# Two merged edits in a Swin block: scores of heads 4 and 5 spread over the whole array, and the narrow half of the second MLP product in rounded passes

## The chip, the cores and the metric

The kernel runs on one core of a Trainium2 chip. The metric is the device time of one execution in microseconds. A core has TensorE (PE, with its weight loads listed apart as PEld), VectorE (DVE), ScalarE (ACT), GpSimd (POOL), and SyncE (SP), which here only issues DMAs. Each engine runs its instructions in order; they meet at semaphores.

## What is computed

One transformer block with shifted 7x7 windows on an input of 16 x 56 x 56 x 192, in float32:

```python
xn = layernorm(x, ln1_w, ln1_b); xs = jnp.roll(xn, (-3, -3), (1, 2))
qkv = windows(xs) @ qkv_w + qkv_b                      # 1024 windows, 49 tokens, 6 heads of 32
attn = softmax(einsum('bhqd,bhkd->bhqk', q, k) * 32 ** -0.5)
o = einsum('bhqk,bhkd->bhqd', attn, v) @ proj_w + proj_b
x = x + roll(unwindow(o), (3, 3), (1, 2))
h = gelu(layernorm(x, ln2_w, ln2_b) @ mlp_w1 + mlp_b1)  # 192 -> 768
out = x + h @ mlp_w2 + mlp_b2                           # 768 -> 192
```

## The kernel before, in words

The work is cut into 128 groups, each a row of eight windows: 392 tokens, held as 4 blocks of 98. `body(i, parity)` of every engine handles the attention of group i and the MLP of group i - 1. `iterations` writes the first three bodies and the last ones out and puts the others, in pairs, into a hardware loop. There is no scheduler: the order on each engine is the order of the calls in its `body`, and the waits are written by hand.

Most products are done in float32 that is split in two. A value is rounded to `float32r` (the high part, by ScalarE or GpSimd) and the rest is the low part (by VectorE or GpSimd); three passes, high x high, high x low and low x high, one record of the trace each, stand for a float32 product. Other products (scores, probabilities times values, the transposes, and the narrow MLP half before) are plain float32 and show two records for a `matmul`.

TensorE's body is, in order:
- `s(i)`: the scores, 32 rows x 64 columns of the array for a product. Heads 0 to 3 read `qA`, `kA` on partitions 0 to 127; heads 4 and 5 read `qB`, `kB` on partitions 64 to 127, in two of the four row parts.
- `transposes2` of the normalised x2 of group i - 1, then `v(i)`, then `mlp1(prev)`: for hidden chunks 0 to 3 passes 0 to 2 of each, then passes 3 and 4 of each, which wait for `zl2_done` from VectorE's `low_narrow2`; then chunks 4 and 5.
- `turn_probs(i)`: 12 transposes of the normalised probabilities. The first half waits for GpSimd's `normalise`, the second for VectorE's.
- `transposes1`, `mlp2_wide` on hidden chunks 0 and 1, `pv(i)`, `mlp2_narrow`, `mlp2_wide` on chunks 2 and 3, `proj(i)`, `mlp2_wide` on chunks 4 and 5, `qk(i + 1, ...)` with the tile of heads 4 and 5 first, and `turn_result(prev)`.

`mlp2_wide` gives output features 0 to 127 in 18 rounded products of 392 columns. `mlp2_narrow` gives the other 64 in float32: 12 products of 196 columns, the even blocks on array columns 0 to 63 and the odd ones on 64 to 127.

VectorE's body is: `scores(i, 0)` (8 slots of 49), `low_wide2`, `scores(i, 1)` (16 slots), `low_narrow2`, `apply1(i + 1)`, `row_sums` twice, `normalise` of half 1, `stats1(i + 2)`, `low_parts1(i + 1)`, the low parts of the attention output (`ol`), the residual, its statistics, `norm_apply` to `z2`, and `result(prev)`. ScalarE makes the high parts, exponentials, GELUs and copies out of PSUM, and rounds GELU chunks 0 to 2 (`high_gelu`); GpSimd rounds chunks 3 to 5 (L385), makes all six low parts (L387), and raises the variances to the power -1/2 (`rstd`, L374).

The lines around the change, before:

```python
for q, k, heads, row, col in ((qA, kA, (0, 1, 2, 3), 0, 0), (qB, kB, (4, 5), 64, PAIRS * TOK)):   # s, L812
...
last = pe.matmul(ps[64 * odd:64 * odd + 64, Y[1], 0:M // 2], w2[:, k, A:C],                      # L871
                 blocks_of(g[:, k, :], odd), start=(k == 0), stop=(k == KC - 1))
```

Of the kernel before, what the change touches and what calls it, by code (L numbers as in the profile page):

```python
# [7 lines left out]
ALU = mybir.AluOpType  # L8
# [27 lines left out]
SLOTS = (0, 1, 2, 4, 3, 5)  # L36
TILES = 2 * HEADS
OUTER = 8


def swin_kernel(nc, x, ln1_w, ln1_b, qkv_w, qkv_b, proj_w, proj_b, ln2_w, ln2_b, mlp_w1, mlp_b1, mlp_w2,
                mlp_b2, out):
    with ExitStack() as ctx:
# [14 lines left out]
        w2l = sb("w2l", [128, KC, A], F32R)  # L58
        wqkv = sb("wqkv", [128, 4, 3 * C], F32R)
# [22 lines left out]
        qB = sb("qB", [128, N + WIDE - EVEN])  # L82
        kA = sb("kA", [128, N])
        kB = sb("kB", [128, N])
# [20 lines left out]
        yTb = sb("yTb", [128, M // 2])  # L105
        yo = sb("yo", [PART, 2, BLOCKS, C])
# [6 lines left out]
        S = (4, 5, 0, 1, 0, 1)  # L113
# [36 lines left out]
        qk_ready = sem("qk_ready")  # L150
        v_done = sem("v_done")
# [123 lines left out]
        ACT_HIGH = 3  # L275
# [69 lines left out]
        def _(pool):  # L345
# [8 lines left out]
            pool.memset(qB[:, N:], 0.0).then_inc(pads_ready, 1)  # L354
# [57 lines left out]
        def _(dve):  # L412
# [44 lines left out]

            def stats1(grp, parity):
# [33 lines left out]
            offset_bias(0, ((128, slice(Q0, QK1 + 1)), (B, slice(V1, V1 + 1))))  # L492
            stats1(1, 1)
# [7 lines left out]
            def low_mlp_weights():  # L501
                low_weight(W1, [(w1[:, 2 * part + 1, :], raw_w1[:, part, :], w1[:, 2 * part, :], lnw[:, 1, part:part + 1])
                                for part in range(2)])
                low_weight(W2, [(w2l[:, :, :], w2[:, :, 0:A], w2h[:, :, :], None)])

            def scores(i, part):

                if part == 0:
                    slots, src = slice(0, OUTER), ps[:, S[0]:S[1] + 1, 0:PAIRS * TOK]
                    wait(dve, pt_done, 2, i - 1, 2)  # L510
                else:
                    slots, src = slice(OUTER, 2 * TILES), ps[:, S[2]:S[3] + 1, 0:2 * PAIRS * TOK]
                wait(dve, s_done, 2, i, part + 1)
                src = src.rearrange("p r (q k) -> p r q k", k=TOK)
                peak, p = mx[:, slots], prob[:, slots, 0:TOK]
                n = slots.stop - slots.start
# [4 lines left out]
                                      .broadcast_to([128, 2, n // 2, TOK]), ALU.subtract).then_inc(s_sub, 1)  # L521
# [17 lines left out]

            def row_sums(i, half):  # L540

                wait(dve, p_exp, 2, i, 2)
# [5 lines left out]
            def body(i, parity):  # L548
# [9 lines left out]
                if more(i):  # L558
                    apply1(i + 1, 1 - parity)
# [3 lines left out]
                if attends(i):  # L563
                    row_sums(i, 0)
                    row_sums(i, 1)
                    normalise(dve, i, 1)
                if more(i + 1) and attends(i):
                    stats1(i + 2, parity)
                if more(i):
                    low_parts1(i + 1)  # L570
                if attends(i):
# [5 lines left out]
                                      by_window_parity(oh[0:64, 1, :]).bitcast(F32), ALU.subtract).then_inc(ol_ready, 1)  # L577
                if not feeds(i):
                    low_mlp_weights()
                if attends(i):  # L580
# [7 lines left out]
                    norm_stats(x2[:, parity, :, :], st2, mv2, bn2, mv2_done, i)  # L588
                    z2_pieces = []
# [12 lines left out]
        def _(act):  # L602
# [409 lines left out]
```

## Time and profile before

| | |
|---|---|
| median of 3 runs | 3097.42 us (3097.29 to 3098.63) |
| profiled execution, its own time | 3099.09 us |
| its span, first to last instruction | 3097.3 us |
| mean granted TensorE clock over the span | 0.993 |
| busy: PE, PEld, DVE, ACT, POOL | 3028.4, 2796.9, 2188.6, 2156.2, 1651.1 us |

Time outside the span is 1.8 us. Matmuls overlap, so a busy TensorE is not a TensorE at its peak; where its order and its spacing of starts show no gap, it is bound by its own work.

### The profile page before, as it was taken

To read this page: it belongs to the slowest core of one execution; us is meant where nothing else is said; L and a number is where in the kernel's file an instruction comes from. 1 tells how busy PE (TensorE), PEld (TensorE's weight loads), DVE (VectorE), ACT (ScalarE), POOL (GpSimd) and SP (SyncE) were. 2 spreads that over 40 slices of the span, in tenths; PEclk is the share of its full clock that TensorE was granted. 3 is DMA by queue.
4 is the path that set the end of the run, shared out by engine and by line. 5 is a ranking of instruction groups with operands and counts; after the bars stand their busy time and mean duration, and the time that the engine had idled before them with its cause. 6 is when DMAs were issued, how large, how long until landed. Compare 5 with 4: busy or idle time off the path is not lost.

```text
span 3097.3 us, 117137 instructions
## 1 busy us (share of the span) xinstructions
PE 3028.4 (98%) x44980; PEld 2796.9 (90%) x44980; DVE 2188.6 (71%) x5903; ACT 2156.2 (70%) x4108; POOL 1651.1 (53%) x1934
## 2 busy tenths in 40 slices
PE   5999999999999999999999999999999999999997
PEld 5899999999999999999999999999999999999996
DVE  4677777777777777777777777777777777777764
ACT  2776776777677677767767776776777677677765
POOL 1555555555555555555555555555555555555553
PEclk8999999999999999999999999999999999999999
DMA  1000100010010001001000100100010010001000
GB/s 46 26 24 23 29 25 23 26 28 23 23 29 25 23 26 29 24 23 29 25 23 26 29 24 23 29 26 23 25 29 24 23 29 26 23 24 30 24 24 17
DMA packets 112148, 79.81 MB, mean 26 GB/s; under 512 B 10129, under 2 KB 111603, under 8 KB 112115
## 3 DMA queue, kind: packets, MB, share of 16 engines
q1 hardware_dynamic: 112114, 79.35, 9.5%
q8 instruction: 23, 0.38, 0.1%
q14 instruction: 11, 0.08, 0.0%
HBM read 40.78 MB, written 38.54 MB: 26 GB/s over the span
## 4 chain that ended last, share of the span: by engine, by line
PE 95%; issue 2%; DVE 1%; POOL 1%; ACT 0%; DMA 0%; SPq 0%; POOLq 0%; DVEq 0%; ACTq 0%
PE ps L785 34%; PE ps L788 15%; PE ps L871 9%; PE ps L896 6%; PE ps L858 5%; PE ps L822 5%; PE ps L862 4%; PE ps L859 4%; PE ps L916 4%; PE ps L748 3%; PE ps L756 2%; PE ps L881 2%; PE ps L884 1%; PE ps L758 1%; DMA xin<-in_x 0%
## 5 line engine op out<-in xcount | busy, mean ns | idle before, releaser
L387 POOL TENSOR_TENSOR gl<-g,gh 128x392 fp32r<-128x392 f32 x768 | 781.2, 1024 | 148.1 <-ACT gh L652 117.1
L785 PE MATMUL ps<-zh,w 128*128 128x392 f32 x3072 | 713.5, 347 | 0.6 <-ACT zh L613 0.6
L785 PEld LDWEIGHTS ps<-zh,w 128*128 128x128 f32 x3072 | 532.1, 188 | 31.4 <-ACT zh L613 0.8
L260 POOL TENSOR_TENSOR prob<-prob,rcp 128x588 f32<-128x588 f32 x128 | 152.6, 1192 | 684.0 <-DVE rcp L546 684.0
L646 ACT ACTIVATE g<-ps,biasf 128x392 f32<-128x392 f32 x768 | 389.5, 574 | 2.2 <-PE ps L785 2.2
L364 POOL TENSOR_TENSOR xb<-xin,projbv 98x768 f32<-98x768 f32 x128 | 234.7, 1834 | 284.8 <-DVE z L430 254.4
L785 PE MATMUL ps<-zh,wqkv 128*128 128x400 f32 x1536 | 376.7, 354 | 0.0
L668 ACT ACTIVATE yT<-ps,b 128x392 f32<-128x392 f32 x128 | 75.4, 589 | 427.8 <-PE ps L862 427.8
L417 DVE BATCH_NORM_STATS2 st<-xin 98x6 f32<-98x192 f32 x512 | 145.8, 347 | 317.3 <-DMA xin<-in_x 317.3
L430 DVE TENSOR_SCALAR z<-x,mv,rs 98x192 f32<-98x192 f32 (+2 forms) x768 | 208.4, 342 | 187.6 <-POOL rs L374 187.6
L526 DVE TENSOR_TENSOR x<-ps,xb 98x384 f32<-98x384 f32 x256 | 142.6, 557 | 253.2 <-PE ps L788 253.2
L785 PEld LDWEIGHTS ps<-zh,wqkv 128*128 128x128 f32 x1536 | 289.5, 190 | 2.7
L858 PE MATMUL ps<-gh,w2h 128*128 128x392 f32 x768 | 289.2, 377 | 0.6 <-POOL gh L385 0.3
L788 PE MATMUL ps<-wqkv,zh 128*114 128x192 f32 x2048 | 287.7, 268 | 0.0
L871 PE MATMUL ps<-g,w 128*64 128x196 f32 x3072 | 284.7, 334 | 1.4 <-issue 1.4
L374 POOL TENSOR_TENSOR rs<-ve,mhalf 98x4 f32<-98x4 f32 x256 | 260.1, 1016 | 20.0
L785 PE MATMUL ps<-zl,w 128*128 128x392 f32 x768 | 261.9, 341 | 0.0
L859 PE MATMUL ps<-gh,w2l 128*128 128x392 f32 x768 | 260.8, 340 | 0.0
L788 PEld LDWEIGHTS ps<-wqkv,zh 128*114 128x114 f32 x2048 | 257.2, 181 | 0.3 <-DVE yo L536 0.2
L788 PE MATMUL ps<-wproj,oh 128*98 128x192 f32 x2048 | 250.4, 253 | 2.6 <-DVE oh L576 2.6
L871 PEld LDWEIGHTS ps<-g,w 128*64 128x64 f32 x3072 | 208.7, 136 | 40.7 <-issue 2.0
L788 PEld LDWEIGHTS ps<-wproj,oh 128*98 128x98 f32 x2048 | 240.4, 164 | 5.4 <-issue 2.4
(101 smaller groups left out, 6843.9 us busy)
## 6 DMA issues: line engine op xcount, KB each, us to landing
xin<-in_x SPq DMA_DIRECT2D x128, 147.0 KB
out<-yo SPq DMA_DIRECT2D x128, 147.0 KB
xin<-in_x SPq DMA_DIRECT2D x128, 71.2 KB
out<-yo SPq DMA_DIRECT2D x128, 71.2 KB
xin<-in_x SPq DMA_DIRECT2D x128, 54.8 KB
out<-yo SPq DMA_DIRECT2D x128, 54.8 KB
xin<-in_x SPq DMA_DIRECT2D x128, 18.8 KB
out<-yo SPq DMA_DIRECT2D x128, 18.8 KB
```

The lines of the kernel that those rows point to most:

```text
L364: pool.tensor_tensor(xb[:, parity, :, :], xin[:, parity, :, :], projbv[:, :].unsqueeze(1).broadcast_to([PART, BLOCKS, C]), ALU.add)\
L374: pool.tensor_tensor(rs[:, :], ve[:, :], mhalf[:, :], ALU.pow).then_inc(rs_done, 1)
L387: pool.tensor_tensor(gl[:, m, :], g[:, m, :], gh[:, m, :].bitcast(F32), ALU.subtract)\
L430: last = dve.tensor_scalar(z, src[:, p, features], mv[:, p, 0:1], rs[:, p:p + 1], ALU.subtract, ALU.mult)
L646: act.activation(g[:, m, :], ps[:, H[m], 0:M], ACT.Gelu, bias=biasf[:, HID0 + m:HID0 + m + 1])\
L785: last = pe.matmul(dst, cols(w, part), act_ if zh is zh2 else windows(act_, WIDE, EVEN), start=(n == 0), stop=(n == 4))
L788: last = pe.matmul(dst, act_[:, tokens], cols(w, part), start=(n == 0), stop=(n == 4))
L822: last = pe.matmul(ps[64 * e:64 * e + 64, S[h], at:at + TOK], q[r, c0:c0 + WIDE], k[r, c0:c0 + TOK], start=True, stop=True)
L858: pe.matmul(dst, w2h[:, k, :], gh[:, k, :], start=(k == 0), stop=False)
L859: pe.matmul(dst, w2l[:, k, :], gh[:, k, :], start=False, stop=False)
L871: last = pe.matmul(ps[64 * odd:64 * odd + 64, Y[1], 0:M // 2], w2[:, k, A:C], blocks_of(g[:, k, :], odd), start=(k == 0), stop=(k == KC - 1))
L896: last = pe.transpose(ps[:, TP[half] + n // 3, 128 * (n % 3):128 * (n % 3) + PAIR], prob[0:PAIR, 2 * b:2 * b + 2, :].rearrange("p w k -> p ...
```

## The change

Scores: keys and queries of heads 4 and 5 are stored with windows 0 to 3 on partitions 64 to 127 and windows 4 to 7 on partitions 0 to 63, so that their 16 products use all four row parts. In `s` the two column halves of a head now follow each other, where before the four heads of one column half did. The scores lie in four banks, `S = (4, 5, 0, 1)`, in two equal halves of 12 slots, with one semaphore at the end. The queries go from ScalarE to VectorE (`queries_45`, new, before `narrow_result`); the order in `pv` follows the new slots.

MLP: the weights `w2s` hold high (columns 0 to 63) and low (64 to 127) of the narrow half. Each chunk is multiplied by the high and by the low part of GELU, in rounded passes of 392 columns; the two column halves of the result are added later: ScalarE copies one with the bias (`yn`), VectorE adds the other (`narrow_result`, two instructions). ScalarE now rounds all six chunks.

Order: on VectorE `apply1` goes behind `normalise`, and `low_parts1` behind the `ol` parts; on ScalarE `high_parts1` goes behind `oh`. The high passes of chunk 4 go ahead of `proj`.

```diff
-                wait(pe, yT_ready, 2, i - 2, 2)
-                for q, k, heads, row, col in ((qA, kA, (0, 1, 2, 3), 0, 0), (qB, kB, (4, 5), 64, PAIRS * TOK)):
-                    for half in range(2):
...
+                for half in range(2):
+                    wait(pe, qk_ready, 2, i, half + 1)
+                    for pair in range(2):
+                        for h in range(4):
+                            scores(S[h], qA, kA, 32 * h, 4 * half, pair, 2 * half + pair)
+                wait(pe, qb_ready, 1, i, 1)
+                for pair in range(2):
+                    for h in range(4):
+                        last = scores(S[h], qB, kB, 32 * h, 0, pair, 4 + pair)
+                last.then_inc(s_done, 1)
...
+            def mlp2(prev, high, low):
...
+                for k in high:
...
+                    pe.matmul(wide, w2h[:, k, :], gh[:, k, :], start=(k == 0), stop=False)
+                    pe.matmul(wide, w2l[:, k, :], gh[:, k, :], start=False, stop=False)
+                    pe.matmul(narrow, w2s[:, k, :], gh[:, k, :], start=(k == 0), stop=False)
+                for k in low:
+                    wait(pe, gl_done, KC, prev, k + 1)
+                    pe.matmul(wide, w2h[:, k, :], gl[:, k, :], start=False, stop=(k == KC - 1))
+                    last = pe.matmul(narrow, w2s[:, k, :], gl[:, k, :], start=False, stop=(k == KC - 1))
...
-                    mlp2_wide(prev, (0, 1))
+                    mlp2(prev, (0, 1), (0, 1))
                 if attends(i):
                     pv(i)
                 if feeds(i):
-                    mlp2_narrow(prev)
-                    mlp2_wide(prev, (2, 3))
+                    mlp2(prev, (2, 3), (2, 3))
+                    mlp2(prev, (4,), ())
                 if attends(i):
                     proj(i)
                 if feeds(i):
-                    mlp2_wide(prev, (4, 5))
+                    mlp2(prev, (5,), (4, 5))
...
+            def queries_45(grp):
+                wait(dve, qk_done, 3, grp, 1)
+                for r, src in ((slice(64, 128), slice(0, N // 2)), (slice(0, 64), slice(N // 2, N))):
+                    last = dve.tensor_scalar(qB[r, 0:N // 2], ps[0:64, QK[2], src], biasf[0:64, QK1:QK1 + 1], None, ALU.add)
+                last.then_inc(qb_ready, 1)
...
+            def narrow_result(prev):
+                wait(dve, yn_ready, 1, prev, 1)
+                for odd in range(2):
+                    last = dve.tensor_tensor(stacked(yTb[64 * odd:64 * odd + 64, :]), blocks_of(ps[0:B, Y[1], 0:M], odd),
+                                             blocks_of(yn[:, :], odd), ALU.add)
+                last.then_inc(yTb_ready, 1)
```

**VectorE, end of a group**, from the statistics of x2 (`st2`, `mv2`) to `z2`. Before:

```order
L422 BN_AGGR mv2<-st2 98x2 [waits bn2]
L422 BN_AGGR mv2<-st2 98x2 x3
L430 TENSOR_SCALAR z2<-x2,mv2,rs2 98x192 [waits mv2_done,rs2_done,t2_done]
L430 TENSOR_SCALAR z2<-x2,mv2,rs2 98x64
L430 TENSOR_SCALAR z2<-x2,mv2,rs2 98x128
L430 TENSOR_SCALAR z2<-x2,mv2,rs2 98x192
L430 TENSOR_SCALAR z2<-x2,mv2,rs2 98x64
L430 TENSOR_SCALAR z2<-x2,mv2,rs2 98x128
L536 TENSOR_TENSOR yo<-ps,x2 98x4x128 [waits ty_done]
L536 TENSOR_TENSOR yo<-ps,x2 98x4x64 [waits ty_done]
```

With the change:

```order
L418 BN_AGGR mv2<-st2 98x2 [waits bn2]
L418 BN_AGGR mv2<-st2 98x2 x3
L458 TENSOR_SCALAR qB<-ps,biasf 64x200 [waits qk_done]
L458 TENSOR_SCALAR qB<-ps,biasf 64x200
L548 TENSOR_TENSOR yTb<-ps,yn 64x196 [waits yn_ready]
L548 TENSOR_TENSOR yTb<-ps,yn 64x196
L426 TENSOR_SCALAR z2<-x2,mv2,rs2 98x192 [waits mv2_done,rs2_done,t2_done]
L426 TENSOR_SCALAR z2<-x2,mv2,rs2 98x64
L426 TENSOR_SCALAR z2<-x2,mv2,rs2 98x128
L426 TENSOR_SCALAR z2<-x2,mv2,rs2 98x192
L426 TENSOR_SCALAR z2<-x2,mv2,rs2 98x64
L426 TENSOR_SCALAR z2<-x2,mv2,rs2 98x128
```

Four instructions now stand between the statistics and `z2`: the queries, and the addition to `yTb`.

**VectorE, after the last low part of the MLP input.** Before:

```order
L454 TENSOR_TENSOR zh2<-ps,zh2 64x2x98 [waits zh2_done] x2
L430 TENSOR_SCALAR z1<-xin,mv1,rs1 98x192 [waits mv1_done,rs1_done,t1_done]
L430 TENSOR_SCALAR z1<-xin,mv1,rs1 98x192 x3
L543 TENSOR_REDUCE psum_row<-prob 128x12 [waits p_exp]
L546 RECIPROCAL rcp<-psum_row 128x12 [waits p_sum]
L543 TENSOR_REDUCE psum_row<-prob 128x12 [waits p_exp]
L546 RECIPROCAL rcp<-psum_row 128x12 [waits p_sum]
L260 TENSOR_TENSOR prob<-prob,rcp 128x12x49 [waits p_rcp]
```

With the change:

```order
L450 TENSOR_TENSOR zh2<-ps,zh2 64x2x98 [waits zh2_done] x2
L555 TENSOR_REDUCE psum_row<-prob 128x12 [waits p_exp]
L558 RECIPROCAL rcp<-psum_row 128x12 [waits p_sum]
L555 TENSOR_REDUCE psum_row<-prob 128x12 [waits p_exp]
L558 RECIPROCAL rcp<-psum_row 128x12 [waits p_sum]
L263 TENSOR_TENSOR prob<-prob,rcp 128x12x49 [waits p_rcp]
L426 TENSOR_SCALAR z1<-xin,mv1,rs1 98x192 [waits mv1_done,rs1_done,t1_done]
L426 TENSOR_SCALAR z1<-xin,mv1,rs1 98x192 x3
```

The four instructions that make `z1` for the next group stand behind the row sums and the normalising now.

**TensorE, from `pv` to the first product of `proj`.** Before (the tail of the first `mlp2_wide` at the top):

```order
L862 MATMUL ps<-gl,w2h 128x392 x2
L916 MATMUL ps<-pt,vt 32x7x7 x48
L871 MATMUL ps<-g,w2 64x196 x12
L858 MATMUL ps<-gh,w2h 128x392
L859 MATMUL ps<-gh,w2l 128x392
L858 MATMUL ps<-gh,w2h 128x392
L859 MATMUL ps<-gh,w2l 128x392
L862 MATMUL ps<-gl,w2h 128x392 x2
L788 MATMUL ps<-wproj,oh 98x192 x2
L788 MATMUL ps<-wproj,ol 98x192
```

With the change, from `pv` on:

```order
L929 MATMUL ps<-pt,vt 32x7x7 x48
L878 MATMUL ps<-gh,w2h 128x392
L879 MATMUL ps<-gh,w2l 128x392
L880 MATMUL ps<-gh,w2s 128x392
L878 MATMUL ps<-gh,w2h 128x392
L879 MATMUL ps<-gh,w2l 128x392
L880 MATMUL ps<-gh,w2s 128x392
L883 MATMUL ps<-gl,w2h 128x392
L884 MATMUL ps<-gl,w2s 128x392
L883 MATMUL ps<-gl,w2h 128x392
L884 MATMUL ps<-gl,w2s 128x392
L878 MATMUL ps<-gh,w2h 128x392
```

The 12 narrow float32 products are gone; `w2s` products stand between the wide ones, and the high passes of chunk 4 stand ahead of `proj`.

## Rows read from the trace of the kernel before

**Rows 1.** Page: chain that ended last, and one group (busy us, mean ns).

```profile
PE 95%; issue 2%; DVE 1%; POOL 1%; ACT 0%; DMA 0%; SPq 0%; POOLq 0%; DVEq 0%; ACTq 0%
...
L871 PE MATMUL ps<-g,w 128*64 128x196 f32 x3072 | 284.7, 334 | 1.4 <-issue 1.4
```

**Rows 2.** Stretch of four groups: engines' busy us, PEclk, DMA share, GB/s.

```profile
1500.00:1594.40 94.40, 93.80 (x1433) 86.75 (x1416) 68.55 (x187) 67.21 (x129) 51.59 (x61) 1.00 0.09 26
```

**Rows 3.** Timeline of TensorE, one group: start us, us, engine line op out<-in xcount.

```profile
1500.79 2.21 PE L871 MATMUL ps<-g,w 128*64 128x196 f32 x24
1502.93 0.45 PE L858 MATMUL ps<-gh,w2h 128*128 128x392 f32 x1
1503.21 0.34 PE L859 MATMUL ps<-gh,w2l 128*128 128x392 f32 x1
...
1504.11 0.35 PE L788 MATMUL ps<-wproj,oh 128*98 128x192 f32 x2
...
1505.90 0.37 PE L858 MATMUL ps<-gh,w2h 128*128 128x392 f32 x1
...
1509.85 0.60 PE L881 MATMUL ps<-ident,yT 128*98 128x128 f32 x4
...
1510.60 0.85 PE L822 MATMUL ps<-kA,qA 32*64 32x49 f32 x62
...
1511.31 0.66 PE L822 MATMUL ps<-kB,qB 32*64 32x49 f32 x30
1511.90 0.56 PE L756 MATMUL ps<-ident,z 98*128 98x98 f32 x4
...
1514.48 0.54 PE L785 MATMUL ps<-zh,w 128*128 128x392 f32 x2
...
1516.71 1.99 PE L785 MATMUL ps<-zh,w 128*128 128x392 f32 x10
...
1520.31 1.37 PE L896 MATMUL ps<-ident,prob 113*128 113x113 f32 x12 [0.16 <-ACT g L646]
...
1522.14 0.43 PE L858 MATMUL ps<-gh,w2h 128*128 128x392 f32 x1
...
1523.39 1.09 PE L916 MATMUL ps<-pt,vt 49*32 49x49 f32 x96
...
1527.72 0.34 PE L788 MATMUL ps<-wproj,oh 128*98 128x192 f32 x2
```

**Rows 4.** Timeline of VectorE, the same group (bracket: idle before, releaser).

```profile
1506.10 0.56 DVE L526 TENSOR_TENSOR x<-ps,xb 98x384 f32<-98x384 f32 x1 [0.23 <-PE ps L788]
...
1507.94 0.38 DVE L422 BATCH_NORM_AGGREGATE mv<-st 98x2 f32<-98x6 f32 x4
1509.79 1.63 DVE L430 TENSOR_SCALAR z<-x,mv,rs 98x192 f32<-98x192 f32 x6 [1.47 <-POOL rs L374]
...
1515.82 0.73 DVE L454 TENSOR_TENSOR zh<-ps,zh 64x196 fp32r<-64x196 f32 x2
1516.58 1.25 DVE L430 TENSOR_SCALAR z<-xin,mv,rs 98x192 f32<-98x192 f32 x4
...
1519.69 0.97 DVE L260 TENSOR_TENSOR prob<-prob,rcp 128x588 f32<-128x588 f32 x1
```

**Rows 5.** Timelines of GpSimd and the weight loads, where the probabilities are turned.

```profile
1518.85 1.19 POOL L260 TENSOR_TENSOR prob<-prob,rcp 128x588 f32<-128x588 f32 x1 [5.30 <-DVE rcp L546]
...
1520.30 0.29 PEld L896 LDWEIGHTS ps<-ident,prob 113*128 113x128 f32 x3 [0.49 <-ACT g L646]
```

**Rows 6.** Timeline of the start: VectorE's end and the weight load that waited for it.

```profile
10.31 1.25 DVE L430 TENSOR_SCALAR z<-xin,mv,rs 98x192 f32<-98x192 f32 x4 [1.50 <-POOL rs L374]
...
11.67 0.46 PEld L748 LDWEIGHTS ps<-ident,z 98*128 98x128 f32 x3 [11.67 <-issue]
```

**Rows 7.** Timeline of ScalarE, the same group.

```profile
1520.00 0.93 ACT L652 ACTIVATE gh<-g 128x392 fp32r<-128x392 f32 x2
...
1524.74 0.53 ACT L724 ACTIVATE oh<-ps 128x392 fp32r<-128x392 f32 x1
```

More of the change, by code:

```diff
@@ L112, in swin_kernel @@
         V = 2
-        S = (4, 5, 0, 1, 0, 1)
+        S = (4, 5, 0, 1)
         T2 = 6
@@ L588, in body @@
                     norm_stats(x2[:, parity, :, :], st2, mv2, bn2, mv2_done, i)
+                    if more(i):
+                        queries_45(i + 1)
+                if feeds(i):
+                    narrow_result(prev)
+                if attends(i):
                     z2_pieces = []
@@ L717, in body @@
                     gelu(prev, 5)
-                if more(i):
-                    wait(act, v_done, 1, i, 1)
-                    high_parts1(i + 1)
+                    for m in range(3, KC):
+                        high_gelu(prev, m)
                 if attends(i):
@@ L725, in body @@
                     act.activation(by_window_parity(oh[0:64, 1, :]), outputs(1)[0:64], ACT.Copy).then_inc(oh_ready, 1)
+                if more(i):
+                    wait(act, v_done, 1, i, 1)
+                    high_parts1(i + 1)
                 if feeds(i):
@@ L808, in s, with scores @@
             def s(i):
[L810 to L824 removed]
+                def scores(bank, q, k, row, first, pair, at):
+                    for e in range(2):
+                        c0 = (first + 2 * e + pair) * EVEN
+                        last = pe.matmul(ps[64 * e:64 * e + 64, bank, at * TOK:at * TOK + TOK], q[row:row + 32, c0:c0 + WIDE],
+                                         k[row:row + 32, c0:c0 + TOK], start=True, stop=True)
+                    return last
+                wait(pe, yT_ready, 1, i - 2, 1)
+                wait(pe, yTb_ready, 1, i - 2, 1)
+                for half in range(2):
[8 more added lines that the diff above has]
+                last.then_inc(s_done, 1)
             def mlp1(prev):
@@ L904, in pv @@
                 pe.nop(nofuse=True)
-                for half in range(2):
-                    for pp in range(2):
-                        for e in range(2):
-                            for n in range(3):
-                                slot = 3 * half + n
-                                h, b, p = SLOTS[slot], 2 * slot + pp, 2 * pp + e
+                for pp in range(2):
+                    for e in range(2):
+                        for heads in ((0, 1, 4, 2), (3, 5)):
+                            for h in heads:
+                                b, p = PROB_BLOCKS.index((h, pp)), 2 * pp + e
                                 cols = slice(32 * (h % 4), 32 * (h % 4) + 32)
```

131 lines of the change are left out of this document (50 added, 81 removed).

## The prediction

> **What bounds the kernel now.** I read the chain of waits first: 95% of the span is TensorE, 2% issue [rows 1]. The stretch of four groups says the same, 93.80 us of 94.40 busy at full clock, while VectorE has 68.55, ScalarE 67.21 and GpSimd 51.59 [rows 2]. That would make it a kernel bound by TensorE's work alone, so I then laid one group out in time. All times below are counted from P = 1505.90, the start of the MLP products behind `proj`. The period is 23.61 us, from `proj` at 1504.11 to `proj` at 1527.72 [rows 3]. 126 of the 128 groups run all parts, and I multiply by 126.
>
> TensorE before, from P: `turn_result` 3.95, scores 4.70, `transposes2` 6.00, `mlp1` 8.58, its third passes 10.81, `turn_probs` 14.41, `mlp2` 16.24, `pv` 17.49, `proj` 21.82, next P 23.61 [rows 3]. A rounded product takes 0.18 (five from 1503.21 to 1504.11 [rows 3]). The 18 products from 10.81 should end at 14.05, yet `turn_probs` starts at 14.41: **0.36 us of waiting in each group**. The weight load there starts at 1520.30, 0.26 behind the end of GpSimd's `normalise` at 1520.04 [rows 5]; the GELU that the profile names isn't what this half waits for. GpSimd waits for the row sums, these for `apply1` on VectorE. So the real loop is P, residual, statistics, `z2`, soft-maximum, low parts (ended at 10.65), `apply1` (1.25), row sums, GpSimd, `turn_probs`, P [rows 4, 5]. One more place is close: the third passes of `mlp1` start at 10.81 and need VectorE's low parts of 10.65 [rows 3, 4]. With the 0.11 that a weight load took to follow VectorE at the start (11.56 to 11.67 [rows 6]) they could not start before 10.76: 0.05 of slack.
>
> **The narrow MLP half.** Removed: 12 float32 products in 24 records, 2.14 us (1500.79 to 1502.93 [rows 3]). Added: 12 rounded ones of 392 columns, 12 x 0.18 = 2.16. Nothing is won. The product behind the narrow ones starts 0.28 later instead of 0.18 [rows 3], a change of array shape that costs 0.10; `pv` now borders on a wide product and I leave the 0.10 there, at that border.
> By the Trainium skill (TensorEngine Tiling (Array Packing), Key Properties) changing the tiling mode drains TensorE. One change of mode fewer in a group would by that rule be worth the 0.10 too, 13 us in all; the rows give no case of `pv` beside a wide product, so this case does not show it.
>
> **The order of MLP products.** Ten products instead of six before `pv`, 13 instead of the narrow ones and six between `pv` and `proj`, seven instead of six behind `proj`. One product (0.18) moves from ahead of `proj` to behind it.
>
> **The scores.** `qA` starts 62 records in 0.85 less a tail of about 0.22, 10.2 ns each; `qB` 30 in 0.66, 14.7 ns each [rows 3]. With 32 records of `qB` at the first rate 0.14 is saved; the least is nothing, if eight parts don't speed them up. I take 0.14, since `qA` runs on the same eight parts. On TensorE's side the third passes then come to 10.81 + 0.18 - 0.14 = 10.85.
>
> **The probabilities times values** keep their number (96 records, 1.01 us from 1523.39 to the narrow products at 1500.79 + 23.61 [rows 3]), but heads 0 and 4, on the same array columns, now stand two apart instead of at least three. Bounds: nothing, and 96 x 4.5 ns = 0.43, if they slow down as `qB` does. I take 0.05, as six array parts are still in use.
>
> **VectorE, the step that decides.** Statistics of x2 end at 2.42 and `z2` starts at 3.89, 1.47 idle for GpSimd's power [rows 4]. Into this gap go two `queries_45` (64x200) and two `narrow_result` (64x196). The nearest row is the low part on 64 partitions, two of 196 elements in 0.73, so 0.37 each [rows 4]. The first can start when the first `qk` tile ends: 7 x 0.18, five `qk` products of 0.19 (15 of them and six of 0.18 fill 1505.90 to 1509.85 [rows 3]) and a tail of 0.17 (a product lasts 0.34, its successor starts after 0.18) make 2.38, so it starts at about 2.47. 4 x 0.37 gives 3.95, and I add 0.08 for the bias operand and for crossing semaphores: `z2` at 4.03, **0.14 late**. Bounds of one instruction: 0.37, and 0.56, that of a whole 98x384 residual [rows 4]. ScalarE's `yn` is no limit: seven products and a tail end at 1.43, a copy of 392 columns is 0.53 [rows 7], and VectorE comes to `narrow_result` at 3.2. TensorE asks for `yTb` at 3.95 + 0.18 = 4.13, and it is there at 4.03 + 0.11: a tie, and an overrun there would only use slack that the third passes have anyway.
> The equal halves of the soft-maximum cost VectorE nothing: 8 + 16 slots become 12 + 12. The low parts end at 10.65 + 0.14 = 10.79, the third passes start at 10.90.
>
> **The wait that goes.** `apply1` leaves the path, so GpSimd ends at about 14.14 + 0.14 - 1.25 = 13.03. `turn_probs` starts when `mlp1` is done, 10.90 + 3.24 = 14.14. What is late next: `z1`, which now ends at about 15.0 (row sums and normalising took from 1516.58 + 1.25 to 1519.69 + 0.97, 2.83 us, and `apply1` 1.25 [rows 4]: 10.79 + 2.83 + 1.25 = 14.87, and gaps), and `transposes1` needs it behind 12 transposes of 1.37 less a tail of 0.17 [rows 3], at 15.34: covered by 0.3.
>
> **Behind it.** `mlp2` at 14.14 + 1.83 = 15.97 (1520.31 to 1522.14 [rows 3]); ten products 1.25 + 4 x 0.18 = 1.97, so `pv` at 17.94; `pv` 1.01 + 0.05, so 19.00; 13 products 2.34 + 0.10, so `proj` at 21.44; `proj` 1.79 (1504.11 to 1505.90 [rows 3]). Next P at **23.23**. Does `ol` keep up? ScalarE began `oh` at 18.84 [rows 7]; three roundings of 0.47 (0.93 for two [rows 7]) take the place of two `high_parts1` of about 0.53, so it is free at about 19.2, and `pv` ends then too. `oh` at 0.93, `ol` at 2 x 0.56, as the residual has with as many columns [rows 4], and the step to TensorE at 0.11 make 21.36 against 21.44. A tie again, with the cover gone: what comes later here is paid in full.
> GpSimd loses three casts and has its low parts ready before TensorE needs them.
>
> **Sum.** 23.61 - 23.23 = 0.38 a group, times 126 = 47.9 us. The start gets 0.9 longer at most (the high and low parts of `w2s`, 384 columns each on ScalarE and VectorE, by the 0.53 and 0.56 of like sizes [rows 4, 7], less what overlaps). 3099.1 (the profiled execution's own time) - 47.9 + 0.9 = 3052.1; the median of the runs lies 1.7 below that execution, and by it I say 3050.
>
> **The rivals.**
> 1. Forecast, chance 0.50: VectorE's loop paces a group, TensorE waits some 0.05 at the third passes instead of 0.36 at `turn_probs`. 3050, its own range 3040 to 3068 (`z2` between 0 and 0.28 late).
> 2. TensorE alone paces, 0.18: the four instructions fit the gap, the border of `pv` costs nothing. Third passes at 10.85, P at 23.23 - 0.05 - 0.10 - 0.05 = 23.03. 0.58 x 126 = 73, so 3025. For it: the gap of 1.47 is just 4 x 0.37. Against: waits of two engines lie in it.
> 3. **Slower: VectorE's four instructions overrun**, 0.10. At 0.56 each `z2` starts at 2.47 + 2.24 = 4.71, 0.82 late; the third passes at 11.58, P at 12.33 more, 23.91, 0.30 longer: 3136. It decides from `z2` 0.52 late on, about 0.48 for each instruction. For it: they cross partitions, and two read a bias; against: the low parts cross partitions too, at 0.37.
> 4. **The parts of a row don't overlap**, 0.07. The two column halves of a head now follow each other on the same 32 rows. Half as many parts busy at a time, and a record takes twice the 14.7 ns of `qB`: 96 x 29.4 = 2.82 in place of 1.16, third passes at 10.85 + 1.66 = 12.51, P at 24.84: 3252, slower. Against it: the narrow products load the same 128 rows and two column halves in turn; each lasts 334 ns [rows 1] and they start 92 apart (24 in 2.21 [rows 3]), so neighbours on the same rows do overlap.
> By the Trainium skill (TensorE: Matmul & The Clock Gate, Part 3, What overlaps and what doesn't) a weight load overlaps running products only when its row group differs. That is this rival's rule; the overlap of the narrow products speaks against it, though with larger pieces.
> 5. Two or three ties break at once (`yTb`, `ol`, `pv` at its upper bound of 0.43), 0.15: the gain is mostly or all returned, P at 23.45 to 23.65, 3078 to 3103.
>
> **Numbers.** About 0.2%, 6 us, is what a measurement can tell from no change. Faster: 0.50 + 0.18 and half of the fifth case, 0.75; the same: 0.09, from the fifth and third; slower: 0.16, from the third and fourth and a little of the fifth. The range leaves out the third and fourth and the far ends of the second and fifth: 3020 to 3100.
>
> **What would show it.** Right: the wait before `turn_probs` gone; a small one of 0.05 to 0.1 at the third passes of `mlp1`; `z2` waiting hardly at all for GpSimd; the rounded narrow products at 0.18; period 23.2 to 23.3; chain still TensorE by nine tenths. Wrong: `z2` over 0.5 late, scores longer than 1.3 us, or VectorE's `ol` as what `proj` waits for.

## The result and the profile after

| | median us | range | runs |
|---|---|---|---|
| before | 3097.36 | 3091.81 to 3098.63 | 4 |
| changed | 3046.47 | 3044.60 to 3047.59 | 4 |

The ratio is 0.9843, with a 95% interval of 0.9831 to 0.9856: 1.6% faster, 50.9 us. The page of the changed kernel, its span, its engines' busy times and its chain, beside 3028.4, 2796.9, 2188.6, 2156.2 and 1651.1 us of busy time before and [rows 1]:

```profile
span 3044.7 us, 114197 instructions
...
PE 2996.3 (98%) x43444; PEld 2857.5 (94%) x43444; DVE 2376.0 (78%) x6416; ACT 2306.3 (76%) x4493; POOL 1483.4 (49%) x1550
...
PE 97%; SPq 1%; DVE 1%; ACT 0%; issue 0%; POOL 0%; DMA 0%; DVEq 0%; POOLq 0%; ACTq 0%
```

TensorE is still busy for 98% and still nearly the whole chain, VectorE has gained 187 us of work and GpSimd has lost 168. Nothing there tells how 51 us went. The timeline of TensorE in one group does. It answers to [rows 3]; P, the start of the MLP products behind `proj`, is 1505.53 here, and times such as 13.06 are counted from it:

```profile
1503.75 0.34 PE L806 MATMUL ps<-wproj,oh 128*98 128x192 f32 x2
...
1505.53 0.36 PE L878 MATMUL ps<-gh,w2h 128*128 128x392 f32 x1
...
1509.65 0.60 PE L895 MATMUL ps<-ident,yT 128*98 128x128 f32 x4
...
1510.40 0.87 PE L832 MATMUL ps<-kA,qA 32*64 32x49 f32 x63
...
1511.54 0.56 PE L774 MATMUL ps<-ident,z 98*128 98x98 f32 x4
...
1512.12 0.45 PE L806 MATMUL ps<-wqkv,zh 128*114 128x192 f32 x2
...
1514.20 0.54 PE L803 MATMUL ps<-zh,w 128*128 128x392 f32 x2
...
1516.44 1.99 PE L803 MATMUL ps<-zh,w 128*128 128x392 f32 x10
...
1519.70 1.32 PE L910 MATMUL ps<-ident,prob 113*128 113x113 f32 x12
...
1521.48 0.42 PE L878 MATMUL ps<-gh,w2h 128*128 128x392 f32 x1
...
1523.44 1.14 PE L929 MATMUL ps<-pt,vt 49*32 49x49 f32 x96
...
1524.51 0.45 PE L878 MATMUL ps<-gh,w2h 128*128 128x392 f32 x1
1524.79 0.34 PE L879 MATMUL ps<-gh,w2l 128*128 128x392 f32 x1
...
1526.94 0.25 PE L806 MATMUL ps<-wproj,oh 128*98 128x192 f32 x1
```

From `proj` to `proj` it is 23.19, against 23.61. The 18 products of `mlp1` from 1516.44 end at the regular spacing, 3.26 later, in `turn_probs`: the 0.36 is gone. The VectorE rows of the same group, for [rows 4]:

```profile
1505.73 0.56 DVE L530 TENSOR_TENSOR x<-ps,xb 98x384 f32<-98x384 f32 x1 [0.24 <-PE ps L806]
...
1507.57 0.38 DVE L418 BATCH_NORM_AGGREGATE mv<-st 98x2 f32<-98x6 f32 x4
1507.98 0.85 DVE L458 TENSOR_SCALAR qB<-ps,biasf 64x200 f32<-64x200 f32 x2
1508.76 0.71 DVE L548 TENSOR_TENSOR yTb<-ps,yn 64x196 f32<-64x196 f32 x2
1509.50 1.63 DVE L426 TENSOR_SCALAR z<-x,mv,rs 98x192 f32<-98x192 f32 x6
1511.05 1.02 DVE L540 TENSOR_TENSOR yo<-ps,x 98x512 f32<-98x512 f32 x2
...
1515.53 0.73 DVE L450 TENSOR_TENSOR zh<-ps,zh 64x196 fp32r<-64x196 f32 x2
...
1519.14 1.24 DVE L426 TENSOR_SCALAR z<-xin,mv,rs 98x192 f32<-98x192 f32 x4
```

and the one of GpSimd, for [rows 5]:

```profile
1517.40 1.19 POOL L263 TENSOR_TENSOR prob<-prob,rcp 128x588 f32<-128x588 f32 x1 [4.12 <-DVE rcp L558]
```

The gap of 1.47 before `z2` is full to the last, `z2` follows `narrow_result` without a pause. GpSimd's `normalise` ends at 1518.59, 1.11 ahead of `turn_probs`. One thing is new: `v` starts at 1512.12, just behind the end of `yo` at 1512.07. `v` of this group waits for the previous result's `yo`, which frees the bank of PSUM that `v` writes.

A second wait stands where the forecast had put it, at the third passes of `mlp1`. TensorE's weight loads there:

```profile
1516.09 0.19 PEld L803 LDWEIGHTS ps<-zl,w 128*128 128x128 f32 x1
1516.38 1.19 PEld L803 LDWEIGHTS ps<-zh,w 128*128 128x128 f32 x7
```

One load ends at 1516.28 and VectorE's low parts at 1516.26 (`zh`, above), but the next load starts only at 1516.38, 0.11 behind the low parts. The first product of the third passes still starts in its turn; the second follows it after 0.225 us, averaged over 105 groups, and after 0.181 in e12 (below), where the low parts are ready 0.36 ahead. That is 0.04 of waiting in each group. In the kernel before it is 0.219: this wait was there already. The busy shares show neither wait, since by the profile the product before still runs through it; in the changed kernel TensorE counts as busy for all of the 2000 us from 500 to 2500 (columns as in [rows 2]):

```profile
500.00:2500.00 2000.00, 2000.00 (x29277) 1908.64 (x29276) 1593.35 (x4309) 1549.43 (x3021) 1000.60 (x1038) 1.00 0.10 26
```

Where the time went, averaged over some 75 groups of each trace, in ns from the first start of one part to the first start of the next. T2 and T1 are `transposes2` and `transposes1`, probs is `turn_probs`, result `turn_result`, narrow the float32 products of `mlp2_narrow`; a, b and c are the other products of the second MLP product, before `pv`, before `proj` and behind `proj` (in the changed kernel they hold the narrow half too). Experiments are named by their first letters:

| | period | scores | T2 | v | mlp1 | probs | T1 | a | pv | narrow | b | proj | c | qk | result |
|---|---|---|---|---|---|---|---|---|---|---|---|---|---|---|---|
| before | 23585 | 1293 | 504 | 2069 | 5796 | 1212 | 619 | 1244 | 1025 | 2141 | 1180 | 1780 | 1106 | 2848 | 766 |
| changed | 23199 | 1147 | 576 | 2083 | 5504 | 1161 | 620 | 1964 | 1065 | | 2430 | 1786 | 1263 | 2852 | 748 |
| e1 | 23354 | 1293 | 505 | 2070 | 5500 | 1160 | 620 | 1348 | 1025 | 2141 | 1178 | 1800 | 1104 | 2844 | 766 |
| e2 | 23522 | 1148 | 564 | 2083 | 5794 | 1212 | 620 | 1963 | 1066 | | 2411 | 1794 | 1270 | 2851 | 749 |
| e3 | 23267 | 1146 | 654 | 2081 | 5506 | 1161 | 619 | 1242 | 1064 | 2141 | 1174 | 1786 | 1093 | 2853 | 747 |
| e4 | 23288 | 1292 | 505 | 2060 | 5455 | 1160 | 620 | 1962 | 1027 | | 2427 | 1792 | 1280 | 2846 | 861 |
| e5 | 24064 | 1147 | 638 | 2082 | 5509 | 1161 | 619 | 1963 | 1065 | | 2425 | 1788 | 1266 | 3638 | 764 |
| e8 | 23195 | 1147 | 505 | 2061 | 5597 | 1161 | 619 | 1964 | 1065 | | 2423 | 1787 | 1265 | 2852 | 748 |
| e10 | 23703 | 1147 | 539 | 2081 | 5507 | 1161 | 620 | 1965 | 1065 | | 2336 | 1873 | 1812 | 2850 | 747 |
| e11 | 23041 | 1146 | 505 | 2060 | 5476 | 1161 | 620 | 1251 | 1025 | 2141 | 1174 | 1785 | 1096 | 2855 | 748 |
| e12 | 23010 | 1146 | 504 | 2060 | 5464 | 1161 | 620 | 1962 | 1024 | | 2427 | 1784 | 1262 | 2850 | 747 |

The averages differ by 0.386 a group; times 126 that is 48.6 of the 52.6 us between the two profiled executions. The rest is near the two ends, by the timelines of TensorE. The first `turn_probs` comes at 54.56 instead of 55.40. The group with the MLP's weights to prepare takes 26.16 instead of 24.15, 2.0 dearer. The traced execution of before has a group of 25.26 (from 103.14 to 128.40), 1.7 too long. In its last group of attention it has a wait of 2.46 inside `pv`, ahead of the last two records, and its narrow products then take 3.64 instead of 2.14; the changed one's has neither:

```profile
3059.83 0.32 PE L916 MATMUL ps<-pt,vt 49*32 49x49 f32 x2 [2.46 <-issue]
```

### The profile page after: what moved, and what is told of

Its sections match the earlier page's. It is cut to its first block, busy times and chain, and to the rows that moved or that the text cites. A ratio compares the mean times of both kernels' runs of the same rounds, so it can differ in the third digit from the quotient of the medians.

```text
span 3044.7 us, 114197 instructions
## 1 busy us (share of the span) xinstructions
PE 2996.3 (98%) x43444; PEld 2857.5 (94%) x43444; DVE 2376.0 (78%) x6416; ACT 2306.3 (76%) x4493; POOL 1483.4 (49%) x1550
## 4 chain that ended last, share of the span: by engine, by line
PE 97%; SPq 1%; DVE 1%; ACT 0%; issue 0%; POOL 0%; DMA 0%; DVEq 0%; POOLq 0%; ACTq 0%
PE ps L803 35%; PE ps L806 16%; PE ps L878 6%; PE ps L910 5%; PE ps L832 5%; PE ps L883 5%; PE ps L929 4%; PE ps L884 4%; PE ps L880 4%; PE ps L879 4%; PE ps L766 3%; PE ps L774 2%; PE ps L895 2%; PE ps L898 1%; SPq L286 1%; PE ps L776 1%
## 5 line engine op out<-in xcount | busy, mean ns | idle before, releaser
L383 POOL TENSOR_TENSOR gl<-g,gh 128x392 fp32r<-128x392 f32 x768 | 789.5, 1050 | 251.6 <-ACT gh L668 251.3
L668 ACT ACTIVATE gh<-g 128x392 fp32r<-128x392 f32 x768 | 365.1, 533 | 0.0
L680 ACT ACTIVATE yn<-ps,b 64x392 f32<-64x392 f32 x128 | 74.7, 583 | 279.0 <-PE ps L884 279.0
L374 POOL TENSOR_TENSOR ve<-mv,eps 98x4 f32<-98x4 f32 x256 | 51.7, 202 | 445.4 <-DVE mv L418 445.4
L883 PE MATMUL ps<-gl,w2h 128*128 128x392 f32 x768 | 262.8, 342 | 0.1
L884 PE MATMUL ps<-gl,w2s 128*128 128x392 f32 x768 | 261.8, 341 | 0.0
L880 PE MATMUL ps<-gh,w2s 128*128 128x392 f32 x768 | 261.7, 341 | 0.0
```

The lines of the kernel that those rows point to most:

```text
L668: act.activation(gh[:, m, :], g[:, m, :], ACT.Copy).then_inc(gh_done, 1)
L880: pe.matmul(narrow, w2s[:, k, :], gh[:, k, :], start=(k == 0), stop=False)
L883: pe.matmul(wide, w2h[:, k, :], gl[:, k, :], start=False, stop=(k == KC - 1))
L884: last = pe.matmul(narrow, w2s[:, k, :], gl[:, k, :], start=False, stop=(k == KC - 1))
```

## The experiments

The theory: a loop through VectorE paces a group. It runs from P by the residual, the statistics, `z2` and `yo` on VectorE to `v` or to the third passes on TensorE, and from there back to P. `apply1` had stood in it, and taking it out gave the gain. The rivals: the array work (scores, rounded narrow products) gave it, or TensorE paces alone. Each kernel is compared with the kernel before, which was run on the same chip.

**e1: the order alone.** The kernel before, with `apply1` behind the probabilities' work.

```diff
                     low_narrow2(prev)
-                if more(i):
-                    apply1(i + 1, 1 - parity)
 ...
                     normalise(dve, i, 1)
+                if more(i):
+                    apply1(i + 1, 1 - parity)
```

> The kernel before with one edit: VectorE's apply1 stands behind normalise. Theory: the waiting of TensorE before turn_probs (0.36 us a group) goes, since GpSimd's normalise no longer has apply1 ahead of it; nothing else is removed, so a group takes 23.25 to 23.35 us and the time is 3052 to 3065, most of the change's gain without a single product changed. Rival (the gain is from the array work of the scores and the narrow half): no change, 3097.

Measured: 3068.85 (3065.42 to 3070.22), ratio 0.9906 [0.9889, 0.9922], above the range expected. The wait before `turn_probs` is gone (`mlp1` 5.50 instead of 5.80). But 0.10 is back in `mlp2` ahead of `pv`. TensorE there:

```profile
1506.92 1.32 PE L896 MATMUL ps<-ident,prob 113*128 113x113 f32 x12
...
1508.70 0.43 PE L858 MATMUL ps<-gh,w2h 128*128 128x392 f32 x1
...
1509.50 0.62 PE L862 MATMUL ps<-gl,w2h 128*128 128x392 f32 x2
```

the weight loads' waits (us in all, times, longest), and GpSimd:

```profile
PEld ps L862 <- POOL gl L387: 16.6, 92, 0.8
```

```profile
1507.52 3.08 POOL L387 TENSOR_TENSOR gl<-g,gh 128x392 fp32r<-128x392 f32 x3 [1.56 <-ACT gh L652]
```

GpSimd's low parts come too late for TensorE: they begin 0.60 behind `turn_probs`, because ScalarE's rounding and the GELU ahead of it are late. In e3 below, which has the same GpSimd work but the equal softmax halves, they begin 0.43 behind `turn_probs` (1521.03 against 1520.60) and nothing waits. ScalarE's last exponential has 784 columns in e1 and takes 0.87, 588 in e3 and 0.71. ScalarE runs without a pause behind it, and that 0.16 is the difference. So 29 of the 51 us need no more than the order. The equal halves of the soft-maximum, which I had costed at nothing, are by these two traces what lets the rest of the order's gain through; no run has them alone.

**e2: the order undone.** The changed kernel with `apply1` back in its old place (e1's diff, reversed).

> The changed kernel with apply1 back ahead of the row sums. Theory: GpSimd's normalise ends 1.25 us later, at 14.3 us from P, turn_probs starts 0.26 behind it at 14.57 instead of 14.17, a group takes 23.6 and the time is 3095 to 3100: the whole gain is gone. Rival (array work): it stays at 3046 to 3055.

Measured: 3084.68 (3082.67 to 3085.52), 0.9958 [0.9941, 0.9974]. The wait is back; GpSimd and TensorE:

```profile
1512.85 1.19 POOL L263 TENSOR_TENSOR prob<-prob,rcp 128x588 f32<-128x588 f32 x1 [5.30 <-DVE rcp L558]
```

```profile
1514.28 1.38 PE L910 MATMUL ps<-ident,prob 113*128 113x113 f32 x12
```

`normalise` ends at 1514.04 and `turn_probs` follows 0.24 later. Scores are 0.145 shorter and `mlp1` again 5.79: with the wait in place the scores' saving is eaten. So the order is needed for three quarters of the gain. Yet 13 us stay, where I had expected at most 2. The stretch from `turn_probs` to P, which belongs to this loop, is 9.07 instead of 9.20 (probs to `proj` in the table), because one product stands behind `proj` now. Against that stands `z2`, which comes 0.07 later, so 0.06 is left in a group, 8 us of the 13; the others lie outside the regular groups. The move of one product, which I had booked without a price, has one whenever VectorE's loop paces.

**e3 and e4: one half of the array work each**, with the new order. e3 is the changed kernel with the MLP of before, e4 the changed kernel with the scores of before.

> The changed kernel with the MLP of before (narrow half in float32, GpSimd rounds chunks 3 to 5, six products before pv): scores and order alone. Theory: 12 rounded products take as long as 24 records, so the MLP part is worth nothing, and the time is that of the changed kernel within 6 us, 3040 to 3052. Rival (the rounded passes carry a part of the gain, by a change of array shape that goes): 3058 or more.

> The changed kernel with the scores of before (heads 4 and 5 in two row parts, 8 and 16 slots, both tiles by ScalarE): MLP and order alone. Theory: the scores last 1.30 instead of 1.14 us, and 0.07 of that is hidden by the wait that v has for yo in the changed kernel, so 0.09 a group more, 3052 to 3064. Rival (TensorE waits for nothing in the changed kernel): the full 0.16 a group more, 3066.

Measured: e3 3055.26 (3053.51 to 3058.53), 0.9867 [0.9851, 0.9884]; e4 3056.85 (3054.71 to 3059.68), 0.9870 [0.9854, 0.9887]. Neither half alone gives it all, and e3 lies between its two expectations. In e3 `narrow_result` is gone from VectorE, and still it is slower. VectorE and TensorE:

```profile
1510.40 1.63 DVE L430 TENSOR_SCALAR z<-x,mv,rs 98x192 f32<-98x192 f32 x6 [0.58 <-issue]
1511.94 1.02 DVE L543 TENSOR_TENSOR yo<-ps,x 98x512 f32<-98x512 f32 x2
```

```profile
1512.75 0.33 PE L766 MATMUL ps<-ident,z 98*128 98x98 f32 x2
1513.01 0.44 PE L796 MATMUL ps<-wqkv,zh 128*114 128x192 f32 x2
```

`yo` ends at 1512.96 and `v` starts at 1513.01: it waits about 0.15 for it (T2 0.654). The loop that paces runs through P, `yo`, `v` and round to P, and its second part holds one product more, ahead of `proj`. Moving the product gives 0.16, the two `narrow_result` take back 0.09 (without them VectorE waits for most of that time, the 0.58 above): net 0.068 a group, 8.6 us, about what lies between e3 and the change (8.8). In e4 the scores take 0.145 more on TensorE, the waits at `v` and at the third passes vanish (`v` and `mlp1` are 0.07 shorter together, T2 0.07), and one of 0.11 on average appears ahead of the scores, where ScalarE makes both tiles. `pv`, which has its old order too, gives 0.04. The sum is 0.09, which is what had been expected, but the 0.11, the 0.04 and the wait at the third passes had not been in the reasoning: that it came out is partly luck.

**e5: `queries_45` done twice**, the second time into a tile that nothing reads.

```diff
+                if not isinstance(grp, int) or grp > 0:
+                    for r, src in ((slice(64, 128), slice(0, N // 2)), (slice(0, 64), slice(N // 2, N))):
+                        last = dve.tensor_scalar(qx[r, :], ps[0:64, QK[2], src], biasf[0:64, QK1:QK1 + 1], None, ALU.add)
                 last.then_inc(qb_ready, 1)
```

> The changed kernel in which VectorE makes the queries of heads 4 and 5 a second time, into a tile that nobody reads (0.78 to 0.85 us more between the statistics of x2 and z2). Theory: VectorE's chain from the end of proj to yo paces the group, since v waits for yo (0.07 us a group in the changed kernel), so all of it is paid: 23.95 to 24.05 us a group, 3140 to 3155. Rival (TensorE paces and VectorE has cover): clearly less than 100 us more, below 3120.

Measured: 3154.41 (3152.12 to 3156.82), 1.0194 [1.0179, 1.0210]. VectorE and TensorE:

```profile
1511.57 0.85 DVE L459 TENSOR_SCALAR qB<-ps,biasf 64x200 f32<-64x200 f32 x2
1512.44 0.85 DVE L462 TENSOR_SCALAR qx<-ps,biasf 64x200 f32<-64x200 f32 x2
1513.21 0.71 DVE L552 TENSOR_TENSOR yTb<-ps,yn 64x196 f32<-64x196 f32 x2
```

```profile
1514.03 0.61 PE L899 MATMUL ps<-ident,yT 128*98 128x128 f32 x4 [0.62 <-issue]
```

0.85 us more work on an engine that is busy for 78% makes the group 0.865 longer. This is the strongest witness for the loop, and it shows rival 3's mechanism and price: at 0.56 for each of the four instructions `z2` would have started at 4.71, 0.74 later than it did, and by this price a group would have taken 23.94 instead of 23.20: the change would have lost. The wait stands ahead of `turn_result`, for `yTb`, and again at `v`.

**e6 and e7: two orders of small pieces.** e6 gives `pv` the old order, in which heads 0 and 4 stand apart; e7 makes the scores go through four heads before the other column half.

```diff
-                for pp in range(2):
-                    for e in range(2):
-                        for heads in ((0, 1, 4, 2), (3, 5)):
+                for heads in ((0, 1, 2), (4, 3, 5)):
+                    for pp in range(2):
+                        for e in range(2):
```

> The changed kernel with the products of pv in the order of before (three heads of different array columns at a time, first half and then second). Theory: pv takes 1.025 instead of 1.065 us, as before the change, and it lies on every path, so 0.04 x 126 = 5 us less, 3041. Rival (the 0.04 is the border to a wide product instead of a narrow one): no change, 3046.

> The changed kernel with the scores in the order of before inside a pair: the four heads of one column half, then those of the other. Theory: array parts on the same rows overlap as well as parts on different rows, so the scores take 1.15 us in either order and the time is 3046 within 4. Rival (a weight load waits for a running product on the same rows): the scores get clearly shorter, by 0.1 us or more, of which the wait of v for yo hides all, so the trace decides: 1.05 or less.

Measured: e6 3039.43 (3038.28 to 3040.16), 0.9821 [0.9808, 0.9835]: `pv` takes 1.024 instead of 1.065, so the order had cost 0.04 a group. That is 5 us, and e6 lies 5 to 7 us below the change (by its two measurements). TensorE in e6:

```profile
1520.44 1.09 PE L929 MATMUL ps<-pt,vt 49*32 49x49 f32 x96
...
1521.46 0.45 PE L878 MATMUL ps<-gh,w2h 128*128 128x392 f32 x1
```

e7 3045.82 (3042.70 to 3047.42), 0.9840 [0.9825, 0.9855]. TensorE in e7:

```profile
1510.25 0.87 PE L833 MATMUL ps<-kA,qA 32*64 32x49 f32 x63
...
1511.40 0.56 PE L774 MATMUL ps<-ident,z 98*128 98x98 f32 x4
```

The scores take 1.15 whether neighbours share their rows or not (1.147 in the changed kernel, 1.146 in e7), so rival 4 is refuted. The rule beside it, of the Trainium skill (TensorE: Matmul & The Clock Gate, Part 3, What overlaps and what doesn't), does not hold for these pieces: had each second piece waited for the one before, which lasts 0.22, 96 records could not have started within 1.15.

**e8: the wait at `v` split by bank.**

```diff
-                wait(pe, yo_done, 2, i - 2, 2)
                 for p in range(PAIRS):
+                    if p % 2 == 0:
+                        wait(pe, yo_done, 2, i - 2, 1 + p // 2)
```

> The changed kernel in which v waits for the first part of yo before its first two pairs (bank 2) and for the second part only before the last two (bank 3), instead of for both at the start. Theory: the 0.07 us that v waits in each group goes; the third passes of mlp1 tie with VectorE's low parts, so nearly all is won: 23.13 to 23.17 us a group, 3037 to 3043. Rival (that wait was covered or another takes its place at once): 3046.

Measured: 3046.87 (3043.01 to 3047.59), 0.9842 [0.9829, 0.9855]: nothing gained, a miss. VectorE and TensorE:

```profile
1516.82 0.73 DVE L450 TENSOR_TENSOR zh<-ps,zh 64x196 fp32r<-64x196 f32 x2
```

```profile
1513.34 0.42 PE L806 MATMUL ps<-wqkv,zh 128*114 128x192 f32 x2
...
1517.47 0.34 PE L803 MATMUL ps<-zl,w 128*128 128x392 f32 x1
1517.70 2.03 PE L803 MATMUL ps<-zh,w 128*128 128x392 f32 x10
```

`v` no longer waits (T2 0.505), and the 0.07 stands where the forecast had put it: the third passes start at 1517.70, behind the low parts that end at 1517.55, and 0.23 behind the product before instead of 0.18, and the second of them loses another 0.03 (`mlp1` 5.597, 0.09 longer). Removing one wait of a loop moved it to the next place where the loop meets TensorE.

**e10: the second tie, `ol`.** One more product group, the high passes of chunk 4, goes behind `proj`.

```diff
                     mlp2(prev, (2, 3), (2, 3))
-                    mlp2(prev, (4,), ())
 ...
-                    mlp2(prev, (5,), (4, 5))
+                    mlp2(prev, (4, 5), (4, 5))
```

> The changed kernel with the high passes of chunk 4 behind proj (ten products ahead of proj, ten behind it, none added or removed). Theory: proj can't start earlier than now, because ol ties with it, so the three products (0.54 us) leave a gap ahead of proj and are all paid behind it, less the 0.07 that v waits: 23.6 to 23.7 us a group, 3095 to 3107. Rival (VectorE's chain from proj to yo paces alone, as experiments 1 to 8 have it, and ol has cover): more work behind proj only fills a wait, 3037 to 3046.

Measured: 3108.58 (3107.13 to 3109.90), 1.0045 [1.0029, 1.0061]. VectorE and TensorE:

```profile
1508.19 0.57 DVE L584 TENSOR_TENSOR ol<-ps,oh 128x392 fp32r<-128x392 f32 x1 [1.30 <-ACT oh L741]
1508.79 0.56 DVE L586 TENSOR_TENSOR oh<-ps,oh 64x392 fp32r<-64x392 f32 x1
```

```profile
1509.40 0.42 PE L806 MATMUL ps<-wproj,oh 128*98 128x192 f32 x2 [0.28 <-DVE oh L586]
```

`ol` ends at 1509.35 and `proj` starts at 1509.40 where 1508.96 was its turn: 0.44 of waiting, and the group grows by 0.50. The tie at `ol` is real, and with 0.54 us less cover it breaks. The time is 1.6 us above the range expected. The trace also shows why more work behind `proj` is not free: the first `qk` tile comes later by the same three products, `queries_45` waits for it (it starts at 2.96 from P instead of 2.45), and `z2` and `v` come 0.51 later.

**e11 and e12: a shorter loop.** If VectorE's chain from P to `z2` paces, it must help to shorten it. The statistics of the first two blocks go between the two residuals, where VectorE waits for `proj`'s second half; e8's split and e6's order are added. e11 has the MLP of before, e12 that of the change, with `narrow_result` ahead of `queries_45`.

```diff
                         residual(i, parity, half)
-                    wait(dve, x2_done, 2, i, 2)
-                    norm_stats(x2[:, parity, :, :], st2, mv2, bn2, mv2_done, i)
+                        wait(dve, x2_done, 2, i, half + 1)
+                        for p in (2 * half, 2 * half + 1):
+                            last = dve.bn_stats(st2[:, p, :], x2[:, parity, p, :])
```

> Scores and order alone (the MLP of before), with VectorE's chain shortened: the statistics of the first two blocks stand between the two residuals, where VectorE waits 0.24 us for proj; v waits for yo in two parts; pv in its old order. Theory: TensorE waits nowhere, 23.08 us a group, 3028 to 3037, the same as the next kernel within 5, since the rounded narrow passes save TensorE nothing. Rival (the rounded passes do save): 10 us or more above the next kernel.

> The changed kernel with the same three edits, and narrow_result ahead of queries_45, which now would have to wait for qk. Theory: z2 starts by 0.2 to 0.35 us earlier, the waits at v and at the third passes are gone, pv takes 1.025: 23.09 us a group, 3030 to 3037. Rival (another chain, by way of ol or ScalarE, paces as well): 3040 or more.

Measured: e11 3026.34 (3022.79 to 3031.10), 0.9781 [0.9766, 0.9795]; **e12 3021.61 (3020.52 to 3023.32), 0.9762 [0.9749, 0.9776]**, 2.4% faster than before and 23 to 25 us below the change (by its two measurements). Both did better than expected. VectorE in e12, with P at 1517.84, 1.78 behind `proj` at 1516.06:

```profile
1517.25 0.56 DVE L530 TENSOR_TENSOR x<-ps,xb 98x384 f32<-98x384 f32 x1
1517.84 0.62 DVE L601 BATCH_NORM_STATS2 st<-x 98x6 f32<-98x192 f32 x2
...
1521.52 1.63 DVE L426 TENSOR_SCALAR z<-x,mv,rs 98x192 f32<-98x192 f32 x6
```

`z2` starts 3.68 behind P instead of 3.97. T2 is back at 0.504 (0.576 in the change), `v` at 2.060 (2.083) and `mlp1` at 5.464 (5.504): together 0.135 a group, which are the waits at `v` and at the third passes. In e12 `yo` ends 0.27 ahead of `v` and the low parts 0.36 ahead of the third passes, and no wait of TensorE is left that I can name. e11 and e12 differ by 4.7 us, hardly more than their spread (e11's fastest run is below e12's slowest), with the MLP as the main difference: the parts a, narrow, b and c add up to 5.662 in e11 and 5.651 in e12. The rounded passes save TensorE 0.01.

**e13: the changed kernel once more.**

> The changed kernel itself, for a comparison on the same chip: 3046 within 3.

Measured: 3044.39 (3042.96 to 3046.07), 0.9837 [0.9823, 0.9850], 2 us from the first measurement; a difference between two experiments of less than that says nothing.

## Why the prediction was right, point by point

3050 was said and 3046.47 measured; faster held, and rival 1, the forecast, is the case that came. A group became 0.386 shorter where 0.38 had been forecast. In that agreement is some luck, as two terms were off in opposite directions: `z2` came 0.06 earlier than forecast, and `v` lost time that the forecast had not listed.

1. **The wait that goes: right.** `turn_probs` 14.17 (14.14 forecast), `normalise` ended at 13.06 (13.03). e1 and e2 show that the order of `apply1` does it.
2. **What it is replaced by: right as far as it went, one place missing.** "TensorE waits some 0.05 at the third passes" came true: 0.04 is lost there. But 0.07 is lost at the start of `v`, and 0.02 more inside it, 4.3 us earlier in the group: `yo` waits behind `z2` on VectorE, and `v` waits for `yo`. In the trace before, `yo` was done only 0.07 ahead of `v`, a tie that I had not listed. And the "0.05 of slack" that I gave the third passes of the kernel before was none: its loads there start 0.115 behind the low parts too, and its second product comes 0.04 late. The third passes start at 10.91 (10.90), but by another road: the low parts ended at 10.73, not 10.79, and TensorE came there late by what it had lost at `v`. Both places hang on the same chain (e8).
3. **`z2`: mis-sized.** 3.97, against 3.89 before and 4.03 forecast: 0.08 late, not 0.14. The first of the four starts at 2.45 (2.47), and they take 1.52 from start to start (0.78 for `queries_45`, 0.74 for `narrow_result`) instead of 4 x 0.37 + 0.08 = 1.56. The term that was too large is the 0.08 for the bias and for crossing semaphores: 0.04 of it came. As an addition (e5) a pair of `queries_45` costs 0.87.
4. **The narrow MLP half: right**, 0.178 for each product; a, narrow, b and c were 5.671 and are 5.657.
5. **The border that costs 0.10: right.** Behind `pv` the next product comes at 1524.79, 0.28 after 1524.51, as behind the narrow ones before. One change of array shape fewer was worth at most the 0.014 of point 4, not the 0.10 that the rule beside it would give (of the Trainium skill, TensorEngine Tiling (Array Packing), Key Properties): what TensorE lost behind the narrow products it now loses behind `pv`. Whether it drains at the other borders too, no run here shows.
6. **The scores: right**, 0.146 shorter (0.14).
7. **`pv`: right**, 0.04 dearer (0.05), and needlessly so (e6).
8. **The moved product: missed.** It was counted as a move without a price. By e2 and e3 it takes 0.14 to 0.16 from the part of VectorE's loop that runs through `pv` and `proj`. The sum held it all the same, because the sum was made by positions, `pv` to `proj` and P, not by prices.
9. **`ol`: right.** `proj` is at 21.41 (21.44). `ol` ends 0.15 ahead of it, of which the step to TensorE takes 0.05, and e10 shows how near that is.
10. **The ends: wrong, small.** +0.9 was forecast for the start. The group with the weights costs 2.0 more, the first `turn_probs` comes 0.84 earlier, one-time waits of the traced execution before (2.46, 1.5 and about 1.7) are absent, and the stretch behind the last `proj` is 0.45 longer: together the 4 us by which the profiled executions differ beyond 48.6. What makes the one-time waits is open; the 2.46 stand as "issue" in the profile. The forecast for the profiled execution was 3052.1, 5.6 too high, of which 4.9 are the ends. The 1.7 that I took off for the median made 3050 look better than that: the profiled execution of the changed kernel is itself the median.

Rival 2 (3025) did not come: TensorE does wait, 0.135 a group. With the statistics early and `pv` in its old order (e12) a group takes 23.01, close to the 23.03 of that rival. Rival 3 is refuted for this change and confirmed as a mechanism (e5), rival 4 by e7. Of rival 5 no tie broke by more than the 0.09 at `v`, and that one was not on its list.

## What to carry to other kernels

An engine that is busy for 98% can still be paced by another engine's chain: lay one period out from one product to the next, follow each other engine round it, and list every place where it meets the busy one by less than 0.1 us, the release of buffers included. In such a loop a wait that was removed at one place came back at the next (e8). What shortened the period was work taken off the chain: `apply1` behind (e1), the statistics early (e12), one product moved behind `proj` (e2, e3), though not three (e10). Faster array work gave its full share where the chain runs through it (`pv` in e6) and nothing where it stands beside the chain (the scores: 0.145 shorter in e3, with 0.15 of waiting in its place). A busy share near 100% shows none of this: a short wait hides in the tail of the product before it.

## What was unexpected of the hardware

- The step from VectorE's end to TensorE is steady at one place and differs between places. The first product of `v` started 54 ns behind the end of `yo`, within 1 ns, and that of `proj` 54 ns behind `ol` in e10. At the third passes the weight load started 115 ns behind the low parts, like the 0.11 at the start of the kernel [rows 6], in every kernel that waited there. For `yTb` in e5 it was 101 ns to the product. Behind GpSimd's `normalise` the first product of `turn_probs` came 0.244 later, with a spread of 0.010, in the kernel before.
- A wait costs TensorE more than its first product shows. Where `v` waited, its second product came after 0.182 instead of 0.162; at the third passes the first product was on time and the second 0.04 late.
- Scores of 32 rows and 64 columns run at the same rate in either order of rows and columns (1.147 and 1.146), so pieces on the same rows overlap too.
- The new order of `pv` costs 0.04 us over 96 pieces (e6). In it heads 0 and 4, on the same array columns, follow each other after two pieces instead of three; that this is the reason is argued, since the order differs in other ways too.
